# A small product over 128 partitions with zero weight rows in place of 64 partitions, in a fused four-layer graph network

## The reference

```
h = relu(layernorm(x))
for k in 0, 1:  h = tanh(concat(adj @ h, h) @ L0_W[k])     # sweeps 1 and 2
x = x + h
h = relu(layernorm(x));  x = x + adj @ (h @ L1_weight) + L1_bias          # sweep 3
h = relu(layernorm(x));  x = x + adj @ (h * (u >= 0.1) / 0.9)             # sweep 4
h = relu(layernorm(x))
x = x + concat(h, adj @ h / (rowsum(adj) + 1)) @ L3_W.T                  # sweep 5
```

## Time and profile before

| | |
|---|---|
| median of 3 runs | 2517.81 us (2514.95, 2517.81, 2521.81) |
| span of the profiled execution | 2515.3 us, from its first to its last instruction |
| TensorE matmul busy | 99% of the span, 7872 instructions |
| weight loads | 43% |
| VectorE / ScalarE / GpSimd | 40% / 5% / 2% |
| DMA | 326 GB/s mean over the span |
| mean granted TensorE clock | 0.993 of full |

### The profile page before, as it was taken

One profiled execution on the slowest core, in us unless ns is written; L12 is line 12 of the kernel. 1 busy time (PEld: TensorE's weight loads), 2 busy tenths in 40 slices (PEclk: granted clock), 3 DMA queues, 4 the chain that ended last, 5 costly groups with the idle time before them and its releaser, 6 DMA issues.

```text
span 2515.3 us, 20176 instructions
## 1 busy us (share of the span) xinstructions
PE 2478.4 (99%) x7872; PEld 1088.2 (43%) x7872; DVE 1002.7 (40%) x1888; ACT 127.6 (5%) x222; POOL 53.4 (2%) x86
## 2 busy tenths in 40 slices
PE   6999999999999999999999999999999999999999
PEld 2334444344444554444444444444444444444444
DVE  7745445444433211010058776877421100006212
ACT  1000000000001211010000000000000000000000
POOL 1000000000000000000000000000000000000000
PEclk9999999999999999999999999999999999999999
DMA  9999989899896677878878878887899999999996
GB/s 389 421 398 368 356 334 365 334 347 334 329 349 226 235 258 275 286 275 291 291 288 308 322 273 301 305 305 269 293 373 362 363 364 351 360 368 366 363 395 264
DMA packets 117791, 820.61 MB, mean 326 GB/s; under 512 B 13505, under 2 KB 17985, under 8 KB 18497
## 3 DMA queue, kind: packets, MB, share of 16 engines
q1 hardware_dynamic: 113904, 814.79, 85.9%
q10 hardware_dynamic: 3024, 2.43, 0.3%
q0 software_dynamic: 768, 2.10, 0.3%
HBM read 817.17 MB, written 2.10 MB: 326 GB/s over the span
## 4 chain that ended last, share of the span: by engine, by line
PE 96%; DVE 2%; DMA 1%; SPq 0%; issue 0%; ACT 0%; DVEq 0%; ACTq 0%
PE double_acc L566 54%; PE single_acc L542 14%; PE spare L566 12%; PE spare L542 8%; PE natural L611 4%; PE natural L616 3%; PE spare L627 1%; PE spare L590 1%; DMA resid<-in_x 1%; DMA ring<-in_adj 1%; DVE centred L714 0%; SPq L499 0%; DVE stats L702 0%; DVE deg_part L744 0%; DVE deg_part L743 0%
## 5 line engine op out<-in xcount | busy, mean ns | idle before, releaser
L566 PE MATMUL double_acc<-ring,operand 128*128 128x512 f32 x3144 | 1377.7, 596 | 2.1 <-DVE operand L834 1.2
L566 PEld LDWEIGHTS double_acc<-ring,operand 128*128 128x128 f32 x3144 | 590.3, 190 | 735.1 <-issue 727.8
L542 PE MATMUL single_acc<-ring,operand 128*64 128x512 f32 x1504 | 358.5, 614 | 26.6 <-DVE operand L728 23.3
L778 DVE TENSOR_TENSOR sums<-double_acc,sums 64x512 f32<-64x512 f32 x60 | 41.3, 689 | 756.6 <-PE double_acc L566 756.4
L566 PE MATMUL spare<-ring,operand 128*128 128x512 f32 x672 | 299.5, 598 | 0.0
L744 DVE TENSOR_TENSOR deg_part<-deg_part,ring 128x1024 f32<-128x1024 f32 x214 | 262.1, 1225 | 7.3
L743 DVE TENSOR_TENSOR deg_part<-deg_part,ring 128x1024 f32<-128x1024 f32 x214 | 261.5, 1222 | 5.3
L790 DVE TENSOR_TENSOR partial<-spare,partial 128x512 f32<-128x512 f32 x115 | 79.5, 691 | 394.9 <-PE spare L566 246.9
L542 PEld LDWEIGHTS single_acc<-ring,operand 128*64 128x64 f32 x1504 | 100.5, 139 | 239.6 <-issue 208.0
L566 PEld LDWEIGHTS spare<-ring,operand 128*128 128x128 f32 x672 | 124.6, 190 | 166.0 <-issue 166.0
L542 PE MATMUL spare<-ring,operand 128*64 128x512 f32 x728 | 164.3, 601 | 1.0 <-DVE partial L790 1.0
(11 more groups left out here) (53 smaller groups left out, 572.8 us busy)
## 6 DMA issues: line engine op xcount, KB each, us to landing
ring<-in_adj SPq DMA_DIRECT2D x756, 1024.0 KB, 6.1
held<-in_adj SPq DMA_DIRECT2D x17, 1024.0 KB, 8.9
resid<-in_x SPq DMA_DIRECT2D x16, 128.0 KB, 15.5
kept<-in_adj SPq DMA_DIRECT2D x2, 1024.0 KB, 8.7
for_layer<-in_u POOLq DMA_DIRECT2D x16, 128.0 KB, 2.5
out_rows<-for_layer ACTq DMA_DIRECT2D x16, 128.0 KB, 5.3
w_both_sb<-in_w_both ACTq DMA_DIRECT2D x1, 160.0 KB, 3.0
w_own_sb<-in_w_own ACTq DMA_DIRECT2D x1, 64.0 KB, 3.2
```

What stands on the lines that cost most here:

```text
L542: last = nc.tensor.matmul(acc[half_of(t % 2), :], operand[:, b.j * TPB + t, half_of(b.row.half)], stream[:, t, :], start=b.first and t < 2 ...
L566: last = nc.tensor.matmul(acc[:, :], operand[:, b.j * TPB + t, :], stream[:, t, :], start=b.first and t == 0, stop=b.last and t == TPB - 1)
L778: nc.vector.tensor_tensor(to, got[own, :], to, ALU.add).then_inc(sums_ready, 1)
```

## The change

The own term's product no longer takes a half of `own_t` and of `w_own_sb`, but all 128 partitions of both. `w_own_sb` gets one column group for each of the sweeps 1, 2 and 5, with the weights in the 64 partitions of that sweep's half and zeros in the other 64. For this GpSimd clears `w_own_sb` first, and ScalarE loads it in three transfers behind the other four constants, once it is cleared. The copy out of the spare bank takes all 128 partitions. The waits for the constants count seven transfers in place of five.

```diff
-        w_own_sb = sb("w_own_sb", [P, 2, F])
+        w_own_sb = sb("w_own_sb", [P, len(WITH_OWN_OPERAND), F])
...
+            pool.memset(w_own_sb[:, :, :], 0.0).then_inc(weights_cleared, 1)
             pool.memset(partial[:, :, :], 0.0).then_inc(cleared, 1)
             pool.memset(operand[:, :, F:2 * F], 0.0).then_inc(cleared, 1)
...
                         last = nc.tensor.matmul(
-                            acc[:, to:to + F], own_t[half_of(row.half), row.r % 2, cut],
-                            w_own_sb[half_of(row.half), row.sweep // SWEEPS, :], start=not mixed, stop=True)
+                            acc[:, to:to + F], own_t[:, row.r % 2, cut],
+                            w_own_sb[:, WITH_OWN_OPERAND.index(row.sweep), :], start=not mixed, stop=True)
...
-            wait_new(consts_loaded, 16 * 5)
+            wait_new(consts_loaded, 16 * 7)
...
-            for to, of in ((w_both_sb, w_both), (w_own_sb, w_own), (bias_sb, bias), (ident, identity), (ones_sb, ones)):
+            for to, of in ((w_both_sb, w_both), (bias_sb, bias), (ident, identity), (ones_sb, ones)):
                 act.dma_start(to[:], of[:]).then_inc(consts_loaded, 16)
+            act.wait_ge(weights_cleared, 1)
+            act.dma_start(w_own_sb[0:F, 0], w_own[0:F, 0]).then_inc(consts_loaded, 16)
+            act.dma_start(w_own_sb[F:P, 1], w_own[F:P, 0]).then_inc(consts_loaded, 16)
+            act.dma_start(w_own_sb[0:F, 2], w_own[0:F, 1]).then_inc(consts_loaded, 16)
...
-                    own = half_of(row.half)
                     use = SPARE_USES.index(("turn", rows_with_own(row.r) - 1))
-                    nc.scalar.copy(own_t[own, slot, :], spare[use % 2][own, :]).then_inc(own_ready, 1)
+                    nc.scalar.copy(own_t[:, slot, :], spare[use % 2][:, :]).then_inc(own_ready, 1)
```

More of the change, by code:

```diff
@@ L442, in gnn_kernel @@
         cleared = sem("cleared")
+        weights_cleared = sem("weights_cleared")
         def data_of(b):
@@ L816, in finish @@
                     dve.wait_ge(u_loaded[slot], 16 * (k // 2 + 1))
-                    dve.wait_ge(consts_loaded, 16 * 5)
+                    dve.wait_ge(consts_loaded, 16 * 7)
                     nc.vector.tensor_scalar(keep[:, :, :], u_in[:, slot], P_DROP, 1.0 / (1.0 - P_DROP),
```

## The result

| | before | after |
|---|---|---|
| median of the runs | 2516.95 us (4 runs, 2514.95 to 2521.81) | 2459.75 us (4 runs, 2458.69 to 2460.79) |
| span of the profiled execution | 2515.3 us | 2458.6 us |
| mean granted clock in it | 0.993 | 0.999 |

The ratio is 0.976, with a 95% interval from 0.974 to 0.979: 57 us faster, where 62.6 were forecast. The time lies inside the range that was given (2447 to 2471), 4.75 us over the value.

The account below looks back on a forecast made before the run. TensorE's own instruction stream was taken as the bound. Terms 50.9 + 15 - 1.0 - 2.3 = 62.6 us off the 2515.3 us span gave 2452.7, and 2.5 us from span to median made 2455 us; range 2447 to 2471.

Parts of the forecast that it names:

- likeliest case: The prediction's own forecast, all its terms together: 62.6 us off the profiled span, 2455 us; chance 0.70.
- (a): Own-term posts of sweeps 1, 2 and 5: all 16 pairs at 128 partitions, 50.9 us gained.
- (b): TensorE's clock: all but one of ten falls behind own-term posts gone, 15 us gained.
- (c): First own post, before the stretch with full DMA queues: its gain only lengthens the wait for blocks, -1.0 us.
- (d): Last sweep: blocks land too late for the earlier TensorE, which then waits 2.3 us.
- (e): Start: GpSimd's extra clear, some 0.2 us, and two more ScalarE transfers are swallowed by first-row waits; cost 0.
- third rival: Own-term posts: pause comes from changing sources or adding products, not from height; nothing removed, 2518 us; chance 0.05.
- first rival: TensorE's clock: the falls stay, only (a) and (c) are left, 2468 us; chance 0.13.
- second rival: Last sweep: DMA queues take over, waits of 8.3 us instead of 2.3, 2461 us; chance 0.08.
- slower rival: The 192 own products: full-height weight loads don't overlap matmuls, +33 us, 2551 us; chance 0.04.

Follow-up runs that it names:

- grouping: Kernel before, 64-partition operands kept, each own post's four products of sums first and four of own_t behind: 2469.49 us, ratio 0.980.
- two versions with a mean clock of 1.000 in every run: Changed kernel with zero rows laid out by the host, plus SHARE 1.7 to 1.5 or AHEAD 6.0 to 10.0: 2454.21 and 2454.28 us.

## Why the prediction was right, and where it was off

The likeliest case came, term by term. In the profiled executions 2515.3 - 2458.6 = 56.7 us were gained against 62.6 forecast.

| term | forecast | measured |
|---|---|---|
| (a) posts at full height | 50.9 | 16 x (0.97 + 1.07 + 0.98) = 48.3 |
| (b) falls of the clock | 15 | 16.6 of the ten that went, less 1.7 of the one at 1740 us: 14.9 |
| (c) first post swallowed | -1.0 | -1.0 |
| (d) waits in the last sweep | -2.3 | -3.3 by starts (-2.4 as counted) |
| (e) start | 0 | -1.5, within the scatter |
| waits for VectorE's operand | 0 | -0.9 |
| sum | 62.6 | 56.5 |

*(a), mis-sized by 2.6 us.* What was off is the price of the eight added pairs. It was taken as the mean of the unmixed post, 0.84 us for eight, but that post's first group of two is cheaper (0.17 us to the next start, as the posts of full height show), and the added ones are not first: they cost 0.22 us a group, 0.90 for eight. The mean of a short run was used for its inner part. The eighth pause, which single blocks keep, was in the forecast without its name, since it took the whole post from unmixed posts at the same place. The mechanism stands: grouping shows the pause at each change of height, 0.14 us, and none at a product of 64 partitions as such, and alternating the sources `sums` and `own_t` costs nothing once both have 128 partitions. That takes the third rival.

*(b), right in size, in part by luck.* All ten falls behind own posts are gone, where the forecast left one in; the one that is there lies behind unmixed posts, which the forecast had said never have one. The cause is only half shown: posts as long as before but without pauses have one fall in place of ten, but how much the pauses do in a shorter post stays open. The Trainium skill (TensorE: Matmul & The Clock Gate, "HAM oscillation") ties a fall to idle gaps; here ten stretches in which the profile shows TensorE busy throughout had one, and the first rival, which followed that rule, is out. The one at 1740 us does have short waits ahead of it, of 0.8 and 0.4 us.

*(c) and (d), right in kind.* The first post's gain went into the waits of the second row, and four waits for blocks appeared near the end. They are counted at 2.4 us, against 2.3, but cost 3.3, so (d) was 1.0 us too small. Its rate, 419 GB/s, was not quite reached (407 from 2303 to 2440 us), and the 2 us for the queue's start had no row behind them. That too many loads were left for the time is shown: with fewer left, the waits go, and none appear elsewhere. The second rival (8.3 us) is out.

*(e), mostly not the change's doing as far as can be seen.* The first double block started 1.5 us later, within what the nine kernels scatter. TensorE's first load starts 0.2 to 0.4 us later with the new start, where the clear was forecast at 0.2; in two of three traces it waits for a late transfer, and not for the clear.

*Not in the forecast at all:* 0.9 us of waits for a normalised operand. Line 834 has 0.8 us in two waits, ahead of the first double blocks of sweep 2, and 0.3 in a third, where the kernel before had 0.2 in one: The likely reason, which no run was made for, is that VectorE's chain is what it was and TensorE now comes to it earlier. The prediction called VectorE's work untouched, which it is, but not its distance to TensorE.

*From span to median.* I added 2.5 us, the distance of the first three runs' median to the span. In most runs the time is only 1.8 us above the run's own span (up to 3.0 in a few); the rest most likely was that the other runs of the kernel before had other numbers of falls.

*The slower rival* (loads over all rows don't overlap) needed more than 0.18 us a pair. The pairs stand at 0.11.

The terms that were off, (a), (d), the start and VectorE's waits, all took from the gain, 6 us together. The range had room for them.

## What to carry to other kernels

Where small products alternate between operands of 64 and of 128 partitions, read the distance between starts, not the busy time. Filling the short operand up with zero rows, or grouping the products by height, takes a pause away at each change and costs nothing where the product's time doesn't depend on its height, as here. Both took nearly all falls of the clock away (one and two left, of ten). A gain on the bounding engine brings it nearer to everything that feeds it: count the transfers left in the last stage against the time left, and move some of them ahead. Read a wait, too, from start to start; its counted length can be too short.

## What the runs showed of the hardware

A change between matmuls of 128 and of 64 partitions costs about 0.14 us in f32 at 2.4 GHz, and the step from 128 to 64 weight columns costs on the way out 0.09 (0.31 against 0.22 us); a pair of load and matmul with 128 weight columns and 64 streamed costs 0.112 us at either height. TensorE's clock can fall without any idle gap in the profile, behind posts of 2.8 us of small products with pauses between them, and not every time: ten times behind 48 such posts in the traced execution, and by the mean clock about 9 to 17 times in others. Some 15 of the 18 us by which the kernel before scatters come from that; two versions with a mean clock of 1.000 in every run repeat within 0.5 us. The first double block, which waits for queued blocks, starts anywhere in 1.5 us across the traces of nine kernels, one each, that issue the same blocks up to it.
